# Graph attention's experts: the second products in groups of one expert, taking turns with VectorE's add

## What is computed

```python
h = (x_flat @ W_gat).reshape(M, HEADS, NUM_EXPERTS)
e = leaky_relu(a_src[src] + a_dst[dst], negative_slope=0.2)
e_max = segment_max(e, dst); ee = exp(e - e_max[dst])
agg = segment_sum(h[src] * (ee / denom[dst])[:, :, None], dst)
scores = layernorm(agg + b_gat).reshape(M, HEADS, NUM_EXPERTS).mean(1)
topk_s, topk_i = top_k(scores, 2); w = softmax(topk_s)
for ei in range(4):
    g = where(topk_i == ei, w, 0.0).sum(-1)
    hh = gelu(x @ W1[ei] + b1[ei])
    out = out + g[..., None] * (hh @ W2[ei] + b2[ei])
```

## Time and profile before

| | |
|---|---|
| median of 3 runs | 10941.02 us |
| profiled execution, its time | 10943.08 us |
| its span in the trace | 10941.5 us |
| mean granted TensorE clock | 0.764 of full speed |
| busy: TensorE, VectorE, GpSimd, ScalarE | 62%, 43%, 52%, 27% of the span |
| indirect DMAs of line 2958 | 1024, 972.4 us busy, 894.6 us idle before them |
| matmul records of line 3099 | 1600, 508.2 us busy, 720.3 us idle before them |
| adds of line 3052 | 100, 67.9 us busy, 1599.1 us idle before them |

### The profile page before, as it was taken

How to read it: one execution, slowest core, us unless ns; L and a number is a source line. 1 busy time by engine, 2 the same in 40 slices (tenths; PEclk the granted TensorE clock), 3 DMA queues, 4 the chain that set the end, 5 groups by cost and what they waited for, 6 DMA issues and landing times. The chain is left out here.

```text
span 10941.5 us, 123202 instructions
## 1 busy us (share of the span) xinstructions
PE 6788.2 (62%) x26564; PEld 4905.6 (45%) x26565; DVE 4692.2 (43%) x10894; ACT 2943.2 (27%) x6917; POOL 5713.7 (52%) x6146
## 2 busy tenths in 40 slices
PE   8577777777777877757886455554444645445441
PEld 4355555555555765536774344342333423223221
DVE  6576666666666666655554111111111301212025
ACT  4344444444444111111111232332323201101000
POOL 2255555555555126665554666666666554554642
PEclk9788888888888977877888666666666767667665
DMA  3455555655655332225553333333323411111114
GB/s 129 148 172 167 172 169 171 171 172 171 173 168 169 100 107 76 72 69 153 151 153 112 97 103 105 102 98 88 88 86 88 135 22 33 37 28 40 23 33 154
DMA packets 668184, 1232.84 MB, mean 113 GB/s; under 512 B 168780, under 2 KB 417024, under 8 KB 667891
## 3 DMA queue, kind: packets, MB, share of 16 engines
q0 software_dynamic: 296176, 717.44, 24.2%
q1 hardware_dynamic: 344261, 473.72, 13.7%
q10 hardware_dynamic: 27580, 39.79, 1.0%
HBM read 1087.91 MB, written 150.62 MB: 113 GB/s over the span
## 5 line engine op out<-in xcount | busy, mean ns | idle before, releaser
L970 POOL DMA_INDIRECT e_kv<-KV,e_idx x1712 | 1626.5, 950 | 1360.6 <-PE e_psA L1087 773.6
L2558 POOL DMA_INDIRECT s_x<-XN,s_idx x1712 | 1627.0, 950 | 589.9 <-issue 519.6
L2958 POOL DMA_INDIRECT t_g<-G,t_idx x1024 | 972.4, 950 | 894.6 <-DMA PG<-t_g 537.8
L1646 POOL DMA_INDIRECT SD<-o_pay,o_pos x880 | 930.8, 1058 | 649.5 <-DVEq L46 322.5
L2616 PE MATMUL s_psA<-s_x,s_oh 128*128 128x257 f32 x1712 | 698.8, 498 | 873.9 <-DVE NS L2653 636.5
L2653 DVE TENSOR_TENSOR NS<-s_psA,NS 128x257 f32 x856 | 364.5, 426 | 2019.9 <-DMA hold<-T3D 1290.7
L1071 PE MATMUL e_psQ<-QA,e_oht 128*128 x3424 | 1029.9, 453 | 135.9 <-issue 135.9
L3099 PE MATMUL t_psY<-t_w,t_H 128*128 128x256 f32 x1600 | 508.2, 446 | 720.3 <-issue 695.3
L2616 PEld LDWEIGHTS s_psA<-s_x,s_oh 128*128 128x128 f32 x1712 | 389.6, 244 | 1072.4 <-issue 983.8
L1071 PEld LDWEIGHTS e_psQ<-QA,e_oht 128*128 128x128 f32 x3424 | 740.5, 225 | 284.4 <-issue 158.2
L3052 DVE TENSOR_TENSOR t_y<-t_psY,t_b 128x512 f32<-128x512 f32 x100 | 67.9, 690 | 1599.1 <-DMA G<-m_g 1195.6
(11 more groups left out here) (593 smaller groups left out, 12044.0 us busy)
## 6 DMA issues: line engine op xcount, KB each, us to landing
o_dbf<-DBF SPq DMA_DIRECT2D x128, 512.0 KB
f_w<-in_L_ffn_Wd_dram SPq DMA_DIRECT2D x57, 1024.0 KB
e_relb<-REL SPq DMA_DIRECT2D x107, 512.0 KB
o_dlo<-DLO SPq DMA_DIRECT2D x128, 256.0 KB
e_kv<-KV,e_idx POOLq DMA_INDIRECT x1712
s_x<-XN,s_idx POOLq DMA_INDIRECT x1712
YD<-t_y ACTq DMA_DIRECT2D x50, 512.0 KB
h_yt<-YD SPq DMA_DIRECT2D x10, 2560.0 KB
```

Of the source, the lines that this page charges most:

```text
L970: pool.indirect_dma_start(kv[:, s, t, :], None, k.KV, bass.IndirectOffsetOnAxis(ap=idx[:, s, t:t + 1], axis=0)).then_inc(kv_in[s][g], 16)
L1646: pool.indirect_dma_start(self.k.SD, bass.IndirectOffsetOnAxis(ap=self.pos[:, s, j:j + 1], axis=0), self.pay[:, s, j, :], None).then_inc(s ...
L2558: pool.indirect_dma_start(x[:, s, t, 0:C], None, k.XN2, bass.IndirectOffsetOnAxis(ap=idx[:, s, t:t + 1], axis=0)).then_inc(x_in[s], 16)
L2958: pool.indirect_dma_start(g[:, s, j, :], None, k.G, bass.IndirectOffsetOnAxis(ap=idx[:, s, j:j + 1], axis=0)).then_inc(g_in[s], 16)
```

## The change

The second products are made and added one expert at a time. `psY` becomes two single banks, picked by the parity of the expert. A group is now 4 products of 256 columns (8 matmul records), `y_done` is raised after each, and VectorE's add is 128x256, so that a full group q of experts has 16 adds where it had 8. TensorE's wait before a group of products is for the add of the group just before it. ScalarE's wait for a finished tile is the same wait in the new count.

```diff
-    TE, YB = 4, 3
+    TE, YB = 4, 2
...
-        psY = c.enter_context(nc.psum_tensor("t_psY", [P, YB, 2, 512], F32))
+        psY = c.enter_context(nc.psum_tensor("t_psY", [P, YB, 512], F32))
...
-        HS, YS = MH, 2 * TE
+        HS, YS = MH, EX * TE
...
-                    for h in range(2):
-                        at(dve, y_done, q, YS, 2 * i + h)
-                        if h == 0:
+                    for e_ in range(EX):
+                        at(dve, y_done, q, YS, EX * i + e_)
+                        if e_ == 0:
                             at(dve, y_kept[i], q - 1, 16, 15)
-                        dve.tensor_tensor(y[:, i, 2 * h * C:(2 * h + 2) * C].rearrange("p (e n) -> p e n", e=2), psY[:, (YS * q + 2 * i + h) % YB, :, 0:C],
-                                          b2[:, 2 * h:2 * h + 2, :], ALU.add).then_inc(yc_done, 1)
+                        dve.tensor_tensor(y[:, i, e_ * C:(e_ + 1) * C], psY[:, e_ % YB, 0:C], b2[:, e_, :], ALU.add).then_inc(yc_done, 1)
...
-                    at(act, yc_done, q, YS, 2 * i + 1)
+                    at(act, yc_done, q, YS, EX * i + EX - 1)
...
-                    for h in range(2):
-                        at(pe, yc_done, q, YS, 2 * i + h - YB)
-                        for b in range(2):
-                            e_ = 2 * h + b
-                            for m in range(4):
-                                last = pe.matmul(psY[:, (YS * q + 2 * i + h) % YB, b, 0:C], H[:, 4 * e_ + m, i * P:(i + 1) * P],
-                                                 w2[:, 4 * e_ + m, :], start=(m == 0), stop=(m == 3))
+                    for e_ in range(EX):
+                        at(pe, yc_done, q, YS, EX * i + e_ - 1)
+                        for m in range(4):
+                            last = pe.matmul(psY[:, e_ % YB, 0:C], H[:, 4 * e_ + m, i * P:(i + 1) * P],
+                                             w2[:, 4 * e_ + m, :], start=(m == 0), stop=(m == 3))
                         last.then_inc(y_done, 1)
```

## The result

The changed kernel takes 11117.6 us (median of 4 runs, 11103.88 to 11157.95) against 10949.19 for the kernel before (4 runs, 10939.0 to 10965.19): ratio 1.0159, 95% interval 1.0128 to 1.0189. Forecast were 11138 us and, against the 10941 us known then, 1.018; the time lies in the range. The profiled execution took 11103.88 us with a span of 11101.6, 160 us more than before's 10941.5.

What follows compares the result with a forecast made beforehand. A loop of waits, no engine full, was taken as the bound, the last add releasing the next gathers. Terms 143 + 18 + 30 + 5 = 197 us gave 11138 us, range 11065 to 11340.

Steps and rivals of the forecast that it cites:

- The loop: VectorE's last add of a group, then softmax and chunk store, release the next gather; gathers start 126.0 us apart.
- A turn: TensorE's 8 records of one expert, then VectorE's add, with gaps: 2.57 us at full clock, against 1.73 without turns.
- The cold start: After gathers drain, TensorE's first turns run at half clock: 1.4 turns at 1.7 us more, 2.4 us.
- Turns left at the drain: When the gathers have drained, 11 of 16 turns remain in an ordinary trip: tail 30.7 us instead of 14.5.
- Turns in the slow stretch: While gathers run, a turn's 16 TensorE instructions still complete at 1.40 us each: 22.4 us per turn.
- the slow stretch: Part of a trip while gathers run: TensorE's instructions complete only every 1.40 us, one record per 2.80 us.
- group 0: First group of experts: TensorE and ScalarE alternate at 1.40 us per instruction; 13 turns remain at the drain, +18.4 us.
- The rival by which they would not be slow at all: Without run-ahead, turns during gathers never provoke slow completions; gathers hold the loop, about 10610 us; chance 0.05.
- the low clock: Rival: TensorE's clock stays low through the turns, 4.3 us each; +401 us, 11342; chance 0.20 with cases between.
- nine single trips: Ordinary trips of groups 1 to 4, 6 to 8, 10 and 11: each 15.9 us longer, 143 us in all.
- groups 5 and 9: Groups with two gathers' time in front: 10 turns remain at the drain, +15.1 us each, 30 in all.
- last group: Final group of experts, 8 turns with completions at 1.40 us each: between nothing and 10 us added, 5 taken.

Runs made afterwards that it cites:

- late adds: Kernel before with the last three adds of a group of experts moved behind the next softmax; ratio 1.0001 alone, 116.7 us for one trip in a mixed kernel.
- e12: One kernel giving each group of experts its own banks and waits, old form in groups 0, 5, 9, 12; 11025.23 us beside the kernel before's 11016.58.
- e11: Kernel before with different banks and waits for each group of experts, in one kernel; 9393.0 us beside the kernel before's 9417.37.
- e5: The kernel before run once more, no edit, for its trace; 10954.13 us.
- e7 to e10: Change with wait one expert looser; kernel before with half-tile turns, last three adds late, or a memset behind each gather; ratios 1.0002, 1.0002, 1.0001, 1.0212.

## Why the prediction was right, step by step

**The loop** was read rightly. The moment when VectorE turns to softmax sets the next gather: with turns it comes later and the trip is longer by that; with late adds it comes 9 us earlier and the trip is 8.6 us shorter (116.7 against 125.3).

**A turn** was put at 2.57 us and measured 2.51 at full clock, 4.30 cold against 4.3. Its parts were split otherwise: a burst of 1.99 us and a gap of 0.52, where 1.73 and 0.8 stood. **The cold start** was put at 2.4 us; two cold turns cost 3.6 in trip 1, one costs 1.8 in trip 2, and three cost 5.4 in trips 8 and 9. **Turns left at the drain**: 11, as counted, in trips 1 and 2. The tail of 30.7 us was 29.4 in trip 2 and 31.2 in trip 1 (9095.01 to 9126.21).

**Turns in the slow stretch** do keep the rate of 1.40 us per instruction, as the turns of group 0 with ScalarE had promised: 22.40 us from 9196.36 to 9218.76. The rival by which they would not be slow at all is out under this condition. So is the low clock: the rival's 4.3 us per turn lasted one to three turns of a trip, and the clock was 0.98 behind them. The Trainium skill's page "TensorE: Matmul & The Clock Gate", section "A second HAM failure mode: psum-queue depth-cycling", tells of a kernel in which brief and frequent idling of TensorE between groups of matmuls makes the clock swing between its two levels. The trace does not agree for these turns: with a gap of 0.52 us in each, the granted clock was 0.98 over 23 us.

**The sum** was 197 us and the profiled executions differ by 160; its terms, by trips:

| | forecast | measured |
|---|---|---|
| nine single trips (groups 1 to 4, 6 to 8, 10 and 11) | +143 | +133.5 (mean 125.94 to 140.77) |
| groups 5 and 9 | +30 | +29.2 (197.4 to 213.1, 197.8 to 211.2) |
| group 0 | +18 | +12.8 (268.1 to 280.9 from the first gather on) |
| last group | +5 | -10.4 (103.9 to 93.5) |
| last trip, and all outside the stage | 0 | -5 |

The term furthest off is the last group, by 15 of the 37 us. Its trip took 103.9 and 99.1 us in two traces of the kernel before, 93.5 and 107.9 in two of the change, and 94.7 in e12 with the old form. With one kernel it swings by 4.9 us, with the other by 14.4, so neither the +5 nor the -10 can be put down to the change. In group 0 the drain came 4.3 us earlier after the first gather than before. In single trips it did too, by up to 4.2 us (9235.56 is 87.6 us behind its first gather, where it was 89.8 to 89.9 in every single trip before). Over the nine this makes some 15 us, more than the 9.5 us by which they fell short; the tails, 31.1 us on average against 30.7, give a little back. The prediction left the drain where it was, and why it comes earlier when TensorE has nothing ahead was not tested.

**What the prediction could not know** is that its premise, the slow stretch, is no constant of the machine. Its reading, completions at 1.40 us each, holds for the condition in which the kernel was traced, and that the changed kernel was timed under the same condition is luck. Under the other, the gathers hold the loop whatever the form, with trips of 82 us: the kernel before takes 9400 us, and the turns lie under the gathers in both groups that had them.

## What to carry to other kernels

Two slots with a wait for the last one are one slot: the depth of a ring is in the wait's index, and e12 gives its price here against the kernel before, 14 to 16 us a trip for none ahead, 4 to 6 for one, none for five. What a hand-off costs depends on what follows it; look for the moment that releases the next long transfer and move the work that nobody waits for behind it (the late adds, 8.6 us in one trip; the whole kernel with late adds ran only where nothing is to be gained, ratio 1.0001, so that it beats the kernel before where the slow stretch is, is not shown; nine single trips at 8.6 us would make 77 us, an estimate from one trip). And before a stall is taken for a property of the code, run the same kernel again at another time.

## What the runs showed of the hardware

Under one condition TensorE's completions reach the other engines at one per 1.40 us while gathers are under way, and GpSimd issues the gathers 1.25 us apart; in the kernel before about 30 records had run ahead of them. Under the other no trace has such a stretch, not even in the groups of e11 that keep the old form (0, 5, 9 and 12), though the gathers are issued at the same 1.25 us. The kernel before itself was only timed there, not traced. The 1560 us between the spans of e5 and e11 do not all lie in the stage of the change: here are three groups of earlier stages. In e5, with the slow stretch:

```profile
L970 POOL DMA_INDIRECT e_kv<-KV,e_idx x1712 | 1625.0, 949 | 1386.3 <-PE e_psA L1087 794.3 <-issue 515.4 <-POOL e_idx L967 60.4
L1646 POOL DMA_INDIRECT SD<-o_pay,o_pos x880 | 931.2, 1058 | 629.5 <-DVEq L46 301.7 <-issue 248.4 <-DVEq L1714 79.0
L2616 PE MATMUL s_psA<-s_x,s_oh 128*128 128x257 f32 x1712 | 698.4, 497 | 884.1 <-DVE NS L2653 647.6 <-issue 205.7 <-DMA s_x<-XN,s_idx 30.3
```

The same three groups in e11, without it:

```profile
L970 POOL DMA_INDIRECT e_kv<-KV,e_idx x1712 | 1622.1, 947 | 1212.4 <-PE e_psA L1087 690.3 <-issue 440.5 <-POOL e_idx L967 81.6
L1646 POOL DMA_INDIRECT SD<-o_pay,o_pos x880 | 935.2, 1063 | 321.8 <-issue 268.1 <-DVEq L1714 42.6 <-DVEq L46 10.2
L2616 PE MATMUL s_psA<-s_x,s_oh 128*128 128x257 f32 x1712 | 662.9, 476 | 1113.1 <-DMA s_x<-XN,s_idx 1021.1 <-issue 92.0
```

GpSimd is busy with the transfers for the same time; what falls is the idle time ahead of them, from 1386.3 to 1212.4 us and from 629.5 to 321.8. TensorE's products of line 2616 wait for their own data where they had waited for VectorE's add (647.6 us), with more idle time than before. From its first to its last instruction each of the three groups takes less: 3142 to 2888 us, 1697 to 1390, and 2581 to 2222. The stage of the change, from its first gather to the last softmax, takes 1948 us in e5 and 1374 in e11. These four differences make 1493 of the 1560 us. What makes the condition stays open: both were met on one chip, e7 to e10 without the stretch and e12 with it, so it is not the chip alone.
